# A two-layer graph network on one core: GpSimd's relational tables made during propagation, from rows that go through DRAM

## What is computed

```
h = relu(layernorm(x)) @ W_in + b_in                     # 3125 x 64
w = rsqrt(deg)[row] * rsqrt(deg)[col]                    # per edge
cur = acc = h
for 3 layers: cur = segment_sum(cur[col] * w, row); acc += cur
x = x + (acc / 4) @ W_out + b_out

h = relu(layernorm(x))
W_rel = einsum('rb,bio->rio', w_comp, weight)            # 16 bases, 64 relations
agg = segment_sum((h @ W_rel[etype])[src] * norm, dst)
out = x + relu(agg + h_bias + h @ loop_weight)
```

## Time and profile before

| | |
|---|---|
| median of 3 runs | 986.79 us (985.37 to 989.05) |
| profiled execution, its time | 984.78 us |
| its span | 983.2 us |
| TensorE busy | 785.8 us (80%) |
| VectorE busy | 719.5 us (73%) |
| GpSimd busy | 471.9 us (48%) |
| ScalarE busy | 355.4 us (36%) |
| mean granted TensorE clock | 0.939 of full speed |

### The profile page before, as it was taken

How to read it: one execution, slowest core, us unless ns; L and a number is a source line. 1 busy time by engine, 2 the same in 40 slices (tenths; PEclk the granted TensorE clock), 3 DMA queues, 4 the chain that set the end, 5 groups by cost and what they waited for, 6 DMA issues and landing times.

```text
span 983.2 us, 27231 instructions
## 1 busy us (share of the span) xinstructions
PE 785.8 (80%) x5974; PEld 584.1 (59%) x5975; DVE 719.5 (73%) x2379; ACT 355.4 (36%) x705; POOL 471.9 (48%) x568
## 2 busy tenths in 40 slices
PE   5666666667879999999179899898888888787876
PEld 3234333333558999998057677676666666555555
DVE  7999999998625644435167777777777877887885
ACT  0422577898760000013154444433433332222100
POOL 2186433231000000101377777777777777777773
PEclk8798999999658999999579999999999999999999
DMA  4022457896330000112951221221211111211213
GB/s 123 22 67 67 117 138 141 159 170 144 98 94 6 2 2 1 34 41 87 293 139 51 54 53 51 53 54 51 53 53 52 53 52 52 54 51 53 54 51 93
DMA packets 64853, 73.32 MB, mean 75 GB/s; under 512 B 12804, under 2 KB 53179, under 8 KB 64667
## 3 DMA queue, kind: packets, MB, share of 16 engines
q1 hardware_dynamic: 48362, 37.30, 15.3%
q0 software_dynamic: 16432, 35.29, 14.3%
HBM read 43.85 MB, written 8.22 MB: 53 GB/s over the span
## 4 chain that ended last, share of the span: by engine, by line
PE 34%; DVE 26%; issue 15%; DVEq 10%; POOL 8%; DMA 5%; ACT 2%; SPq 1%; POOLq 0%; ACTq 0%
PE ps L1211 16%; PE ps L1288 10%; POOL CT L677 7%; DVE ohbuf L843 7%; DVE CT L985 5%; DVE u L843 4%; DMA CT<-h_dram,src_col 4%; PE ps L1119 4%; DVE CT L988 3%; DVEq L988 3%; DVEq L127 3%; PE ps L1267 2%; DVEq L985 2%; DVE ohbuf L838 2%; DVEq L843 1%
## 5 line engine op out<-in xcount | busy, mean ns | idle before, releaser
L677 POOL DMA_INDIRECT CT<-h_dram,src_col x391 | 370.5, 948 | 126.7 <-issue 105.4
L1288 PE MATMUL ps<-CT 128*128 128x256 f32 x1180 | 302.6, 405 | 65.4 <-DVE CT L985 31.7
L1288 PEld LDWEIGHTS ps<-CT 128*128 128x128 f32 x1180 | 203.0, 191 | 159.2 <-issue 142.1
L988 DVE SCALAR_TENSOR_TENSOR CT<-ps,dlP,CT 128x256 f32<-128x256 f32 x580 | 279.4, 482 | 4.5
L985 DVE COPY CT<-CT 128x128 f32 x590 | 148.3, 251 | 123.6 <-PE ps L1288 54.7
L1430 ACT COPY CT<-ps 128x256 f32<-128x256 f32 x200 | 77.6, 388 | 307.1 <-PE ps L1288 303.6
L1119 PE MATMUL ps<-ohbuf 128*128 128x400 bf16 x395 | 103.5, 368 | 42.3 <-DVE ohbuf L843 18.6
L1368 ACT CAST stage<-ps 128x800 bf16<-128x800 f32 x100 | 82.3, 823 | 75.6 <-PE ps L1119 74.5
L1211 PE MATMUL ps<-u,CT 128*128 128x192 bf16 x1250 | 105.0, 246 | 0.9 <-DVEq L951 0.9
L1211 PEld LDWEIGHTS ps<-u,CT 128*128 128x128 bf16 x1250 | 103.1, 98 | 1.9 <-DVEq L951 1.1
L843 DVE TENSOR_SCALAR ohbuf<-iota,keys 128x400 bf16<-128x400 int16 x395 | 103.1, 324 | 0.0
(11 more groups left out here) (186 smaller groups left out, 619.5 us busy)
## 6 DMA issues: line engine op xcount, KB each, us to landing
CT<-stage SPq DMA_DIRECT2D x200, 100.0 KB, 3.5
u<-types_dram POOLq DMA_DIRECT2D x49, 128.0 KB, 3.6
CT<-h_dram,src_col POOLq DMA_INDIRECT x391, 2.5
coef_dram<-coef_out POOLq DMA_DIRECT2D x49, 64.0 KB, 3.8
CT<-coef_dram SPq DMA_DIRECT2D x1, 3048.0 KB, 11.0
out<-CT SPq DMA_DIRECT2D x4, 256.0 KB
ohbuf<-x SPq DMA_DIRECT2D x3, 320.0 KB, 3.8
x_dram<-ohbuf SPq DMA_DIRECT2D x3, 320.0 KB, 2.7
```

What stands on the lines that cost most here:

```text
L677: pool.indirect_dma_start(out=gring[:, (j + 1) % GRING, :], out_offset=None, in_=h2_dram, in_offset=bass.IndirectOffsetOnAxis(ap=src_col[: ...
L988: dve.scalar_tensor_tensor(kpair[:, u, :, :], nodes.unsqueeze(1).broadcast_to([P, BASES, WIN]), dl, coef_flat[:, ds(tiles * -BASES + NT * ...
L1288: pe.matmul(ps[:, ds(summed.place(counts[u][0], RING), 1), 0:WIN * BASES], gpair[:, u, :], kpair[:, u, :, :].rearrange("p b d -> p (b d)") ...
```

## The change

The tables are computed in one piece, behind the last coefficient store in GpSimd's program, and GpSimd waits there for `rows_in`. The four rows that they are made from lie side by side in `rows` (946 words). After the types, SyncE stores them to `rows_dram`; behind the last group of `CT` and a wait for `deg_cut` it loads them back into `keys`, whose count-stage contents are no longer needed. Scratch lies in `keys` and `stage`. VectorE makes the row of each turn's last tile itself, with one more copy. The row of differences between neighbouring pairs is gone: the windows themselves are multiplied with other weights and summed. The comparison of 1500 elements becomes 25 comparisons of 60 elements, each followed by an addition. GpSimd's first 12 turns of loads and stores are in its loop. SyncE no longer waits ahead of group 19. ScalarE waits for `rel_tables` ahead of layer 2's first copy, VectorE in that layer's second batch.

```diff
--- before.py
+++ after.py
@@ -69,7 +69,8 @@
 STATS_EARLY = 10
-TAIL_TABLES, TAIL_H = 19, 22
+TAIL_H = 22
+ROWS = S // 2 + TURNS + NW + 1 + NT
 CRING = 6
...
@@ -170,6 +171,7 @@
         types_dram = nc.dram_tensor("types_dram", (TC * P * P,), BF16, kind="Internal").ap()
+        rows_dram = nc.dram_tensor("rows_dram", (1, ROWS), F32, kind="Internal").ap()
         x2_dram = nc.dram_tensor("x2_dram", (NPAD, FEAT), F32, kind="Internal").ap()
...
@@ -278,26 +280,25 @@
-        at[0] = TAIL_TABLES * NPAD // 2
         ts_s = carve(S // 2).bitcast(I16)
-        ws_s = carve(S // 2).bitcast(I16)
         iota_s = carve(S // 2).bitcast(I16)
...
         at[0] = TAIL_H * NPAD // 2
...
         bin_sb = carve(HID)
+        def rows_at(flat):
+            ws, ts = flat[:, 0:S // 2].bitcast(I16), flat[:, S // 2:S // 2 + TURNS]
+            ends = flat[:, S // 2 + TURNS:S // 2 + TURNS + NW + 1]
+            return ws, ts, ends, flat[:, ROWS - NT:ROWS]
+        rows = carve(ROWS)
+        ws_s, ts_last, end_f, tile_f = rows_at(rows)
...
@@ -321,6 +322,26 @@
         zsb = carve2(2 * P * BASES).rearrange("p (h b d) -> p h b d", h=2, b=BASES)
+        at[0] = 0
+        rows2 = carve_keys(ROWS)
+        ws_r, ts_r, ends_r, tile_r = rows_at(rows2)
+        bits = carve_keys(TURNS)
+        ws_last = carve_keys(TURNS)
+        pair_ends = carve_keys(NW // 2)
+        stage_f = stage[:, :, :].rearrange("p r n -> p (r n)").bitcast(F32)
+        at3 = [2 * BATCH * HID]
...
+        ws_f = carve_stage(S)
+        turn_i = carve_stage(TURNS + 1).bitcast(I32)
+        turn_f = carve_stage(TURNS + 1)
+        grp_f = carve_stage(TURNS + 1)
+        begun = carve_stage(TURNS + 1)
...
@@ -353,6 +374,8 @@
         rel_tables = sem("rel_tables")
+        rows_st = sem("rows_st")
+        rows_in = sem("rows_in")
...
@@ -436,6 +459,9 @@
             sp.dma_start(tiles_view(types_dram, 0, TC), type_b).then_inc(types_st, 16)
+            sp.wait_ge(slots_listed, 1)
+            sp.wait_ge(cols_made, 1)
+            sp.dma_start(rows_dram, rows[0:1, :]).then_inc(rows_st, 16)
...
@@ -447,11 +473,13 @@
-            rows_out(0, TAIL_TABLES)
-            sp.wait_ge(rel_tables, 1)
-            rows_out(TAIL_TABLES, TAIL_H)
+            rows_out(0, TAIL_H)
             sp.wait_ge(hadded, H_TURNS)
+            sp.wait_ge(rows_st, 16)
             rows_out(TAIL_H, NG)
+            sp.wait_ge(deg_cut, 1)
+            sp.dma_start(rows2[0:1, :], rows_dram).then_inc(rows_in, 16)
...
@@ -537,7 +565,7 @@
                 pool.memset(weights[:, 0, u:u + 1], float(1 << (BANK_BITS * (u % HU) if u % HU < HU - 1 else LAST_SHIFT))).then_inc(pool_c, 1)
-                pool.memset(weights[:, 1, u:u + 1], float(1 << BASE + u - 1) if u else 0.0).then_inc(pool_c, 1)
+                pool.memset(weights[:, 1, u:u + 1], float(1 << BASE + U - 2) if u == U - 1 else -float(1 << BASE + max(u - 1, 0))).then_inc(pool_c, 1)
...
@@ -560,100 +588,57 @@
-            tabled = [0]
-            def step_t(ins, wait=True):
-                tabled[0] += 1
-                ins.then_inc(pool_t, 1)
-                if wait:
-                    pool.wait_ge(pool_t, tabled[0])
-            turn = lambda row: row[0:1, :].rearrange("p (c u) -> p c u", u=U)
...
-            def moves_of_turns():
-                pool.wait_ge(slots_listed, 1)
-                step_t(pool.memset(moves[0:1, 0:1], 0.0), False)
-                step_t(pool.tensor_copy(ts_last[0:1, :], last_of(ts_s)), False)
-                step_t(pool.tensor_copy(ws_f[0:1, :], ws_s[0:1, :]))
-                step_t(pool.tensor_tensor(moves[0:1, 1:S], ws_f[0:1, 1:S], ws_f[0:1, 0:S - 1], ALU.subtract))
-                step_t(pool.tensor_tensor(turn(moves), turn(moves), weights[:, 1].unsqueeze(1).broadcast_to([1, TURNS, U]),
-                                          ALU.mult))
-            def bits_of_turns():
-                step_t(pool.tensor_copy(bits[0:1, :], last_of(moves)))
-                for u in range(U - 1):
-                    step_t(pool.tensor_tensor(bits[0:1, :], bits[0:1, :], turn(moves)[:, :, u], ALU.add))
...
-                starts = end_f[0:1, 0:NW].rearrange("p (g w) -> p g w", w=WPG)[:, :, 0]
-                step_t(pool.tensor_tensor(grpM[0:1], starts.unsqueeze(2).broadcast_to([1, NG, TURNS + 1]),
-                                          turn_f[0:1, :].unsqueeze(1).broadcast_to([1, NG, TURNS + 1]), ALU.subtract))
-                step_t(pool.tensor_scalar(grpM[0:1], grpM[0:1], 0.0, None, ALU.is_ge))
...
-            def places_of_tiles():
-                pool.wait_ge(cols_made, 1)
-                step_t(pool.tensor_scalar(tab_tile[:], tile_f[0:1, :], -2.0, 2.0 * S, ALU.mult, ALU.add))
-                pool.sem_inc(rel_tables, 1)
             assert (CT_TURNS - 1 - HALVES) % HALVES == 0
-            peeled = 4 * HALVES
-            for c in range(peeled):
-                reload_types(c + 1 + HALVES, (c + 1) % HALVES)
-                store_coefs(c, c % HALVES)
-                if c == 2:
-                    moves_of_turns()
-                if c == 3:
-                    bits_of_turns()
...
-                    words_of_groups()
-                if c == 9:
-                    places_of_tiles()
             pool.addr_align(BLOCK, offset=0, max_nops=0)
-            with pool.Fori(peeled // HALVES, (CT_TURNS - 1 - HALVES) // HALVES) as q:
+            with pool.Fori(0, (CT_TURNS - 1 - HALVES) // HALVES) as q:
                 for j in range(HALVES):
...
+            tabled = [0]
+            def step_t(ins, wait=True):
+                tabled[0] += 1
+                ins.then_inc(pool_t, 1)
+                if wait:
+                    pool.wait_ge(pool_t, tabled[0])
+            turn = lambda row: row[0:1, :].rearrange("p (c u) -> p c u", u=U)
+            before = lambda hi: ends_r[0:1, 0:NW].rearrange("p (w k) -> p w k", k=2)[:, :, hi]
+            pool.wait_ge(rows_in, 16)
+            step_t(pool.iota(turn_i[0:1, :], pattern=[[U, TURNS + 1]], base=-1, channel_multiplier=0), False)
+            step_t(pool.memset(grp_f[0:1, :], 0.0), False)
+            step_t(pool.tensor_copy(ws_f[0:1, :], ws_r[0:1, :]))
+            step_t(pool.tensor_copy(turn_f[0:1, :], turn_i[0:1, :]), False)
+            step_t(pool.tensor_copy(ws_last[0:1, :], turn(ws_f)[:, :, U - 1]))
+            step_t(pool.tensor_tensor(turn(ws_f), turn(ws_f), weights[:, 1].unsqueeze(1).broadcast_to([1, TURNS, U]), ALU.mult))
+            step_t(pool.tensor_copy(bits[0:1, :], turn(ws_f)[:, :, U - 1]))
+            for u in range(U - 1):
+                step_t(pool.tensor_tensor(bits[0:1, :], bits[0:1, :], turn(ws_f)[:, :, u], ALU.add))
+            step_t(pool.tensor_tensor(ws_last[0:1, :], bits[0:1, :], ws_last[0:1, :], ALU.subtract))
+            step_t(pool.tensor_scalar(tab_sum[:, :, 0], ws_last[0:1, :], float(NW), None, ALU.add), False)
+            step_t(pool.tensor_tensor(bits[0:1, :], bits[0:1, :], ts_r[0:1, :], ALU.add))
+            step_t(pool.tensor_scalar(tab_pair[:], bits[0:1, :], -1.0, float(NT + ((1 << U - 1) - 1 << BASE)),
+                                      ALU.mult, ALU.add), False)
+            step_t(pool.tensor_scalar(pair_ends[0:1, :], before(1), float(1 << BASE), None, ALU.mult))
+            step_t(pool.tensor_tensor(pair_ends[0:1, :], pair_ends[0:1, :], before(0), ALU.add))
+            step_t(pool.tensor_scalar(tab_back[:], pair_ends[0:1, :], -1.0, float((S - 1) * (MASK + 2)), ALU.mult, ALU.add),
+                   False)
+            for g in range(NG):
+                step_t(pool.tensor_scalar(begun[0:1, :], turn_f[0:1, :], ends_r[0:1, g * WPG:g * WPG + 1], None, ALU.is_le))
+                step_t(pool.tensor_tensor(grp_f[0:1, :], grp_f[0:1, :], begun[0:1, :], ALU.add))
+            step_t(pool.tensor_scalar(begun[0:1, :], grp_f[0:1, :], 32.0, None, ALU.mult))
+            step_t(pool.tensor_tensor(begun[0:1, 0:TURNS], begun[0:1, 0:TURNS], grp_f[0:1, 1:TURNS + 1], ALU.add))
+            step_t(pool.tensor_copy(tab_sum[:, :, 1], begun[0:1, 0:TURNS]), False)
+            step_t(pool.tensor_scalar(tab_tile[:], tile_r[0:1, :], -2.0, 2.0 * S, ALU.mult, ALU.add))
+            pool.sem_inc(rel_tables, 1)
...
@@ -746,6 +731,7 @@
             dve.sem_inc(tables_in, 1)
+            step(dve.tensor_copy(ts_last[0:1, :], ts_s[0:1, :].rearrange("p (c u) -> p c u", u=U)[:, :, U - 1]), False)
             step(dve.tensor_tensor(ws_s[:], iota_s[:], ts_s[:], ALU.subtract))
...
@@ -958,6 +944,8 @@
                         dve.sem_inc(acc_done, 1)
+                        if b == 1:
+                            dve.wait_ge(rel_tables, 1)
                         if b:
...
@@ -965,7 +953,6 @@
             dve.wait_ge(ld_coef, 16)
-            dve.wait_ge(rel_tables, 1)
             pairs = Turn(dve, "pair", NT)
...
@@ -1404,6 +1391,7 @@
+            act.wait_ge(rel_tables, 1)
             for b in range(NB):
...
@@ -1415,7 +1403,6 @@
-            act.wait_ge(rel_tables, 1)
             act.sem_inc(routed, 2)
...
```

(44 more changed lines are left out.)

39 lines of the change are left out of this document (removed).

## The result

The changed kernel takes **975.89 us** (median of 4 runs, 974.94 to 976.36), the kernel before in the same comparison 986.99 (4 runs, 985.37 to 989.05): a ratio of 0.9881, 95% interval 0.9864 to 0.9899, 11.1 us less. The profiled execution took 974.94 us.

A forecast was written before the change was run, and what follows sets the result against it. No engine was taken to bound the whole span; VectorE is the chain in the count stage, TensorE in propagation. -12.4 us there plus 0.6 in propagation gave -11.8, so 975.0 us, range 971 to 981.5.

The forecast's parts named there:

- -12.38 for the pairs of turns: Count stage: four pairs of VectorE's turns fall from 44.90 to 32.52 us once the table instructions leave.
- 0 for the loop and SyncE's wait: Count stage: GpSimd's first twelve turns moved into its loop, and SyncE's dropped wait for the tables, change nothing.
- 0 for the copy at the start: Setup: VectorE's added copy of 59 elements is covered by its wait for TensorE, 0.3 us if not.
- 2.7 us allowed for the clock: From 243 to 301 us: an earlier start may shift four matmul groups across TensorE's clock change, 2.7 us either way.
- The list, 36 us from 300: Propagation: GpSimd's 77 table instructions run from 300 to 336 us, old time scale, covered by 70 us of slack.
- 1.53 ns each: Old tables' cost to VectorE per element; applied to 6100 new elements in propagation it gave 9.4 us lost, 26%.
- Expected delays 0.5, 2, growing to 4.5: Start of propagation: delays in us of VectorE's six parts, covered by slack of 0.8, 2.2, growing to 8.6.
- 26% of 1.5 us is 0.4: At 321.91 us: TensorE waits for VectorE's three reads of 1.5 us, which lose 0.4 us on the path.
- case 1: Rival: the collision moves to propagation and VectorE's 9.4 us count where TensorE waits, 983.8 us; chance 10%.
- (2): Rival: the gain is partly absorbed before 297 us by low clock or waits on ScalarE, about 981 us; chance 8%.
- (3): Rival: the longer comparisons in the count stage have another source and stay, 986 to 987 us; chance 6%.
- (4): Rival: small instructions in propagation hold VectorE as large ones did, 90% lost, 998.4 us; chance 4%.

The follow-up runs named there:

- e4: The change, with GpSimd's first twelve turns of loads and stores written out and SyncE's row transfers in two loops again: 975.05 us, ratio 0.9881.
- e2: The change, its 25 compares of 60 elements replaced by wide subtractions and comparisons on 600, 600 and 300 elements, still late: 976.89 us, ratio 0.9896.
- e1: The kernel before, with the change's new table list left in the count stage, five pairs a turn in turns 6 to 10: 990.11 us, ratio 1.0029.
- e6: The kernel before, with the new table list in the count stage, two pairs a turn in turns 6 to 18: 977.58 us, ratio 0.9896.
- e7: The kernel before, its two instructions on 1500 elements cut into five of 300 each, same place: 984.30 us, ratio 0.9973.
- e3: The change, with GpSimd's late list started only when VectorE's six parts are made: 975.92 us, ratio 0.988.
- e11: The changed kernel itself, unaltered, run again: 976.42 us, ratio 0.9873 against the kernel before.
- e5: The change, with the 25 compare-and-add pairs ahead of the cast and product on 590 elements in the late list: 974.12 us, ratio 0.9871.

## Why the prediction came true, point by point

- **975.0 against 975.89**, range 971 to 981.5, chance of faster 0.85: right. So were the shape and the signs named to look for: windows of 8.1, the last copy at 96.38 (said 96.2), degrees at 285.73 (said 285), the first 250 matmuls unbroken (20.80 us).
- **-12.38 for the pairs of turns** held, as did 0 for the loop and SyncE's wait (e4). The 0 for the copy at the start didn't quite: it took 0.20 us at 15.65, and the pairs of turns start at 47.49 to 47.62 in the change, e2 and e4, and at 47.21 to 47.41 in before, e1, e6 and e7, which lack it. That is within the 0.3 named as the other end. The stage's end moved by 11.73; from the last copy to the degrees it is 189.35 us against 188.90, at a granted clock of 0.87 and 0.88. Over the kernels of this study it is 188.9 to 193.6 us (e3, at 0.85), more than any edit of the late list moves. The changed kernel's own trace used 0.45 of the 2.7 us allowed for the clock; that of e11, the same kernel, took 192.30 us at 0.83, 3.4 over before. So a step read from two single traces carries some 3 us of this.
- **The list, 36 us from 300**: 38.7 us from 287.58, which is 299.3 on the old scale. The pair at 0.9 was 0.91; the nine sums took 4.82, not 4.04. In cover, as said.
- **"1.53 ns each", hence 9.4 us or 26% lost**: wrong. To 328 us VectorE lost 1.48 us in its first part, 0.2 in its fifth and 0.33 at 325.82. The average over the old tables mixed long two-input instructions, which hold VectorE for nearly their whole time, with others that hardly do. The step took a mean for a law; a price for each kind was needed. The rule cited there from the Trainium skill (GPSIMD Engine Reference, § Key points), that two SBUF inputs suffice for a collision, agrees with lines 898 and 900 beside the cast and product; beside the small ones little was lost (last section).
- **"Expected delays 0.5, 2, growing to 4.5"**: they didn't grow. Nearly all harm fell into the first part, the least covered one: TensorE waited 0.79 us there, where 0.5 less a slack of 0.8 had been counted as nothing. **"26% of 1.5 us is 0.4"** for the reads of the first sums: none, all three 0.49 and the wait 0.87 as before. So 0.6 was near the 0.3 to 0.8 found, by luck: two errors against each other.
- **What gains**, the step that matters most for the next kernel: the prediction credited the move. By e6 the new list alone gives 9.0 us, so the instructions that it drops, the two on 1500 elements and the additions in halves, did most of the harm. The place adds 3.4 us in the windows; in the medians it is 1.7, but these are of two comparisons whose ratios overlap (0.9896 and 0.9881), so the times alone don't show it. e2 is nearly the other half: the wide comparisons late, beside a list otherwise new, cost nothing that can be told. So either edit alone would have brought most of it; for the old list late as it was that is argued, not run.
- **Rivals.** The collision does move (case 1), with 0.8 us on the path and not 9.4. Nothing was absorbed in the count stage (2). The comparisons' length went with the tables (3). Small instructions didn't hold VectorE as large ones did (4): what it lost, 2.0 us in all, is a twentieth of the list's 38.7.
- **The last stage**, from the first gather to the end, took 503.0 us before and 505.3 after. All other kernels lie between these two: 503.8 (e1), 504.9 (e6) and 504.8 (e7) with the tables in the count stage, 504.8 in e11, the change again, 503.6 in e5. Nothing in the diff touches the stage, and these numbers show no step between old and new place; what moves it from one execution to the next is left open.

## What to carry to other kernels

Small computations on GpSimd beside a VectorE that never waits are not free, and what they cost goes by kind and by what stands next to them (an add of 60 elements cost 1.8 ns an element in a row of adds, and with a comparison between each two 0.3): look for two-input and wide ones first, and cut or rewrite them (an accumulation of compare and add) before moving them. Where GpSimd also issues loads, keep what is put between two of them well under a turn: e1 lost the whole gain to loads that came late. A price per element from a mean over unlike instructions is no law; price each kind by its own row. To put the first instructions of a moved list where its neighbour has slack (e3) is sound by the traces; here it was worth less than the times can tell.
